# One attention block and a gated low-rank layer on one core: the last pair of heads takes its rounds upwards and projects four of its units beside itself

## What is computed

```python
q = (x @ wq.T + bq).reshape(B, S, H, hd)      # x is layernorm(x) here; k and v likewise
scores = einsum('bqhd,bkhd->bhqk', q, k) / sqrt(hd)
scores = where(causal, -inf, scores)
attn = einsum('bhqk,bkhd->bqhd', softmax(scores), v).reshape(B, S, D)
x = x + layernorm(attn @ wo.T + bo)
x = x + layernorm(gated_low_rank(layernorm(x)))   # 8 experts, one chosen for each token
```

## Time and profile before

| | us |
|---|---|
| median of 3 runs | 2445.38 |
| profiled execution, its own time | 2448.2 |
| its span, first to last instruction | 2446.4 |
| TensorE busy in the span | 2271.6 (93%) |
| ScalarE busy | 1728.8 (71%) |
| VectorE busy | 1673.9 (68%) |
| GpSimd busy | 1646.6 (67%) |
| mean granted clock of TensorE | 0.974 |

### The profile page before, as it was taken

One profiled execution on the slowest core, in us unless ns is written; L12 is line 12 of the kernel. 1 busy time (PEld: TensorE's weight loads), 2 busy tenths in 40 slices (PEclk: granted clock), 3 DMA queues, 4 the chain that ended last, 5 costly groups with the idle time before them and its releaser, 6 DMA issues. The chain is left out here.

```text
span 2446.4 us, 70598 instructions
## 1 busy us (share of the span) xinstructions
PE 2271.6 (93%) x28626; PEld 1446.4 (59%) x28626; DVE 1673.9 (68%) x4154; ACT 1728.8 (71%) x2355; POOL 1646.6 (67%) x1295
## 2 busy tenths in 40 slices
PE   4899999999999989899999999999997569999995
PEld 2566666675757666567575757666674335445452
DVE  8577777777777766476666666666666536777776
ACT  3477777777777766677777777777777746666665
POOL 4578788888888876678887888787887822222221
PEclk9999999999999999999999999999998779999997
DMA  9699999999999999999999999999999966656653
GB/s 239 130 195 203 200 200 202 202 205 203 204 202 205 203 197 199 199 194 191 185 189 182 185 185 186 185 180 184 174 177 191 204 142 155 160 154 169 156 155 86
DMA packets 1424676, 450.05 MB, mean 184 GB/s; under 512 B 1402048, under 2 KB 1402448, under 8 KB 1424352
## 3 DMA queue, kind: packets, MB, share of 16 engines
q1 hardware_dynamic: 1424352, 445.54, 98.5%
HBM read 67.95 MB, written 41.94 MB: 45 GB/s over the span
## 5 line engine op out<-in xcount | busy, mean ns | idle before, releaser
L911 POOL TENSOR_TENSOR hl<-probs,hl 128x1024 f16<-128x1024 f32 x544 | 1164.1, 2147 | 367.7 <-ACT hl L794 365.6
L787 ACT ACTIVATE probs<-s_ps,exp_bias 128x1024 f32<-128x1024 f32 (+7 forms) x768 | 632.7, 853 | 334.8 <-DVE exp_bias L636 328.2
L631 DVE TENSOR_REDUCE neg_max<-s_ps 128x1 f32<-128x1024 f32 (+7 forms) x768 | 676.1, 905 | 174.7 <-PE s_ps L472 174.6
L794 ACT ACTIVATE hl<-probs 128x1024 f16<-128x1024 f32 x544 | 575.0, 1057 | 70.1 <-DMA pt<-hl 53.9
L472 PE MATMUL s_ps<-nat 64*128 64x512 f16 (+3 forms) x3840 | 414.4, 354 | 75.7 <-ACT probs L787 72.3
L495 PE MATMUL o_ps<-v,pt 128*128 128x65 f16 x4352 | 434.8, 194 | 25.9 <-DMA pt<-hl 16.3
L495 PEld LDWEIGHTS o_ps<-v,pt 128*128 128x128 f16 x4352 | 403.5, 97 | 56.7 <-issue 23.2
L496 PE MATMUL o_ps<-v,pt 128*128 128x65 f16 x4352 | 434.9, 195 | 0.0
L497 PE MATMUL o_ps<-v,pt 128*128 128x65 f16 x4352 | 433.6, 193 | 0.0
L524 PE MATMUL u_ps<-arena,w 128*128 128x512 f16 x1008 | 385.8, 383 | 36.9 <-DMA arena<-hl 35.1
L496 PEld LDWEIGHTS o_ps<-v,pt 128*128 128x128 f16 x4352 | 402.7, 98 | 19.1
(11 more groups left out here) (160 smaller groups left out, 3672.0 us busy)
## 6 DMA issues: line engine op xcount, KB each, us to landing
w_raw<-in_w_pairs SPq DMA_DIRECT2D x48, 576.0 KB, 4.9
o_scratch<-o_hl SPq DMA_DIRECT2D x128, 128.0 KB, 2.5
out<-result SPq DMA_DIRECT2D x32, 512.0 KB, 3.3
x_in<-in_x SPq DMA_DIRECT2D x27, 512.0 KB, 4.9
pt<-hl SPq DMA_TRANSPOSE x544, 5.1
nat<-in_x SPq DMA_DIRECT2D x16, 512.0 KB, 4.6
xn_scratch<-xn SPq DMA_DIRECT2D x16, 512.0 KB, 4.1
xn<-in_x SPq DMA_DIRECT2D x11, 512.0 KB, 4.2
```

The source lines that it names most:

```text
L631: nc.vector.tensor_reduce(neg_max[:, step.round, acc, h:h + 1], s_ps[(n + h) % S_RING][:, first:end], AX_X, ALU.max, negate=True).then_inc ...
L787: last = nc.scalar.activation(probs_of(n)[:, cols], s_ps[n % S_RING][:, cols], ACT.Exp, bias=exp_bias[:, step.round, acc, h:h + 1], scale= ...
L794: nc.scalar.activation(hl_of(n, 0), probs_of(n), ACT.Copy).then_inc(p_hi_done, 1)
L911: nc.gpsimd.tensor_tensor(hl_of(n, 1), probs_of(n), hl_of(n, 0), ALU.subtract).then_inc(p_lo_done, 1)
```

## The change

- Pair 15 takes its rounds in the order of `FIRST_ROUNDS` (upwards), as pair 0 does.
- Eight of pair 15's units are projected during pair 14 (kind "prelast"), each over two steps, in steps 0 to 15. The last four, chunk 3 of k, chunks 0 and 3 of q and chunk 3 of v, are projected during pair 15 itself, in steps 0 to 4 (one, one, one and two steps).
- The weight blocks are summed by VectorE, in `center_wo`, with a reduction and a scaling; ScalarE's `wo_sum` is gone. Block k is summed and centred in body k + 2 (block 7 in body 10), and split by ScalarE and GpSimd in body k + 6, since the arena is in use until the units are done. The two fills of the arena move from body 0 to body 6.
- SyncE loads blocks 0 and 1 in body 0, block i + 1 in bodies 1 to 5, and block 7 in body 8. Of the smaller loads, five that `row_sum` needs are issued in body 7, the other six two a body in bodies 8 to 10 and awaited in body 15.
- `store_rows` stands one body later, in every pair.

```diff
-steps_of = lambda p: STEPS if p else FIRST_STEPS
-rounds_of = lambda p: ROUNDS if p else FIRST_ROUNDS
+upwards = lambda p: p in (0, PAIRS - 1)
+steps_of = lambda p: FIRST_STEPS if upwards(p) else STEPS
+rounds_of = lambda p: FIRST_ROUNDS if upwards(p) else ROUNDS
...
+UNITS["prelast"] = [("k", 0), ("k", 1), ("k", 2), ("q", 2), ("q", 1), ("v", 0), ("v", 1), ("v", 2), ("k", 3), ("q", 0),
+                    ("q", 3), ("v", 3)]
+LATE_UNIT = 8
...
+              "prelast": [2] * LATE_UNIT, "last": [1, 1, 1, 2]}
...
+units_of = lambda p: min(p + 1, PAIRS - 1)
...
-                    if i == half_done(p) + 1:
+                    if i == half_done(p) + 2:
                         store_rows(p, 0)
-                    if p > 0 and i == 1:
+                    if p > 0 and i == 2:
                         store_rows(p - 1, 1)
-                    if kind == "last" and i == 0:
+                    if kind == "last":
+                        for k in ([0, 1] if i == 0 else [i + 1] if i < KT - 2 else []):
+                            if k == 0:
+                                sp.wait_ge(s_done, NTASK * (PAIRS - 1))
+                            if k == 4:
+                                sp.wait_ge(pv_done, NTASK * (PAIRS - 1))
+                            if k == 6:
+                                sp.wait_ge(w_lo_done, 3 * PAIRS)
+                            sp.dma_start(wo_raw[k], fin["w_view"][k]).then_inc(wo_loaded[k], 16)
+                    if kind == "last" and i == KT - 1:
                         sp.wait_ge(unit_done, N_UNIT * PAIRS)
-                        sp.wait_ge(s_done, NTASK * (PAIRS - 1))
                         sp.wait_ge(mix_set, 2)
-
-                    if kind == "last" and i < KT:
-                        if i == 4:
-                            sp.wait_ge(pv_done, NTASK * (PAIRS - 1))
-                        if i == KT - 1:
-                            sp.wait_ge(wo_lo_done, 1)
-                        sp.dma_start(wo_raw[i], fin["w_view"][i]).then_inc(wo_loaded[i], 16)
-                    if kind == "last" and i >= KT:
-                        for tile, source in fin["loads"][4 * (i - KT):4 * (i - KT + 1)]:
+                        for tile, source in fin["row_loads"]:
+                            sp.dma_start(tile, source).then_inc(rows_loaded, 16)
+                    if kind == "last" and i == KT:
+
+                        sp.wait_ge(wo_lo_done, 1)
+                        sp.dma_start(wo_raw[KT - 1], fin["w_view"][KT - 1]).then_inc(wo_loaded[KT - 1], 16)
+                    if kind == "last" and KT <= i < KT + 3:
+                        for tile, source in fin["loads"][2 * (i - KT):2 * (i - KT + 1)]:
                             sp.dma_start(tile, source).then_inc(fin_loaded, 16)
...
             def center_wo(k):
-                raw = wo_raw[k]
+                raw, mean = wo_raw[k], wo_mean[:, k:k + 1]
+                dve.wait_ge(wo_loaded[k], 16)
+                nc.vector.tensor_reduce(mean, raw, AX_X, ALU.add).then_inc(wo_sum_done, 1)
+                dve.wait_ge(wo_sum_done, k + 1)
+                nc.vector.tensor_scalar(mean, mean, 1.0 / D, None, ALU.mult).then_inc(wo_mean_done, 1)
                 dve.wait_ge(wo_mean_done, k + 1)
-                nc.vector.tensor_scalar(raw, raw, wo_mean[:, k:k + 1], W_SCALE, ALU.subtract, ALU.mult).then_inc(
-                    wo_centered, 1)
+                nc.vector.tensor_scalar(raw, raw, mean, W_SCALE, ALU.subtract, ALU.mult).then_inc(wo_centered, 1)
...
-                        if 2 <= i < 2 + KT:
+                        if 2 <= i < 1 + KT:
                             center_wo(i - 2)
+                        if i == 10:
+                            center_wo(KT - 1)
...
             def wo_high(k):
                 act.wait_ge(wo_centered, k + 1)
+                act.wait_ge(unit_done, N_UNIT * PAIRS)
...
             def row_sum(n, row):
-                act.wait_ge(fin_loaded, 16 * len(fin["loads"]))
+                act.wait_ge(rows_loaded, 16 * len(fin["row_loads"]))
...
                 act.wait_ge(fin_centered, 3)
+                act.wait_ge(fin_loaded, 16 * len(fin["loads"]))
...
-                    if kind == "last" and 1 <= i < 1 + KT:
-                        wo_sum(i - 1)
-                    if kind == "last" and 2 <= i < 2 + KT:
-                        wo_high(i - 2)
+                    if kind == "last" and 6 <= i < 6 + KT:
+                        wo_high(i - 6)
...
-                    if kind == "last" and 2 <= i < 2 + KT:
-                        wo_low(i - 2)
+                    if kind == "last" and 6 <= i < 6 + KT:
+                        wo_low(i - 6)
```

More of the change, by code:

```diff
@@ L118 @@
 UNITS["first"] = UNITS["mid"]
-KIND = {0: "first", PAIRS - 1: "last", HALF_PAIRS - 2: "pre", HALF_PAIRS - 1: "turn"}
+UNITS["prelast"] = [("k", 0), ("k", 1), ("k", 2), ("q", 2), ("q", 1), ("v", 0), ("v", 1), ("v", 2), ("k", 3), ("q", 0),
+                    ("q", 3), ("v", 3)]
+LATE_UNIT = 8
+KIND = {0: "first", PAIRS - 1: "last", PAIRS - 2: "prelast", HALF_PAIRS - 2: "pre", HALF_PAIRS - 1: "turn"}
 order_of = lambda p: UNITS["start" if p == 0 else KIND.get(p - 1, "mid")]
@@ L125 @@
 UNIT_STEPS = {"first": [1, 1, 2, 2, 1, 1, 1, 2, 1, 2, 1, 2], "mid": [1, 1, 1, 2, 1, 2, 1, 2, 1, 2, 1, 2],
-              "pre": [1, 1, 1, 2, 1, 1, 1, 2, 2, 1, 2, 2], "turn": [1, 1, 1, 2, 1, 1, 1, 2, 2, 1, 2, 2], "last": []}
-UNIT_AT = {kind: [(u, i, n) for u, n in enumerate(counts) for i in range(n)] for kind, counts in UNIT_STEPS.items()}
-assert all(len(at) in (0, NSTEP) for at in UNIT_AT.values())
+              "pre": [1, 1, 1, 2, 1, 1, 1, 2, 2, 1, 2, 2], "turn": [1, 1, 1, 2, 1, 1, 1, 2, 2, 1, 2, 2],
+              "prelast": [2] * LATE_UNIT, "last": [1, 1, 1, 2]}
+UNIT_AT = {kind: [(u + (LATE_UNIT if kind == "last" else 0), i, n) for u, n in enumerate(counts) for i in range(n)]
+           for kind, counts in UNIT_STEPS.items()}
+units_of = lambda p: min(p + 1, PAIRS - 1)
 SPLITS = {"mid": {2: "q", 5: "k", 14: "v"}, "pre": {2: "q", 13: "k", 16: "v"}, "turn": {2: "q", 13: "k", 16: "v"}}
 SPLITS["first"] = {1: "v", 4: "q", 7: "k", 14: "v"}
-SPLITS["last"] = {}
+SPLITS["prelast"], SPLITS["last"] = {2: "q"}, {}
 last_step = lambda kind, m: max(i for i, (u, part, n) in enumerate(UNIT_AT[kind]) if UNITS[kind][u][0] == m)
@@ L265, in attend_phase @@
         fin_loaded = sem("fin_loaded")
+        rows_loaded = sem("rows_loaded")
         wo_loaded = [sem(f"wo_loaded{k}") for k in range(KT)]
@@ L269, in attend_phase @@
         ffn_hi_done = sem("ffn_hi_done")
+        wo_sum_done = sem("wo_sum_done")
         wo_mean_done = sem("wo_mean_done")
@@ L534, in body @@
                         scores(*step)
-                    if UNITS[kind]:
-                        u, part, count = UNIT_AT[kind][i]
-                        atoms = ATOMS[UNITS[kind][u][0]] // count
-                        project(p + 1, u, part * atoms, (part + 1) * atoms)
+                    for u, part, count in UNIT_AT[kind][i:i + 1]:
+                        atoms = ATOMS[order_of(units_of(p))[u][0]] // count
+                        project(units_of(p), u, part * atoms, (part + 1) * atoms)
                     for h in range(2):
@@ L719, in body @@
                     if kind == "last":
-                        if i == 0:
+                        if i == 6:
                             dve.wait_ge(unit_done, N_UNIT * PAIRS)
@@ L949, in body @@
                     for u in units_ending(kind, i - 1):
-                        unit_low(p + 1, u)
+                        unit_low(units_of(p), u)
                     if step:
@@ L1046, in finish_inputs @@
     fin["load_o"], fin["load_x"] = load_o, load_x
-    fin["loads"] = [(fin["bo_row"][:], b_o.partition_broadcast(P)),
-                    (fin["ffn_w"][:], by_block(ffn_in)),
-                    (fin["probe"][:], by_block(ffn_probe)),
-                    (fin["degen"][0:LOWS], ffn_mix[0:LOWS]), (fin["degen"][LOWS:P], ffn_mix[0:LOWS]),
-                    (fin["bias"][BIAS_HI:BIAS_HI + N_EXP], ffn_mix[LOWS:]),
-                    (fin["bias"][BIAS_LO:BIAS_LO + N_EXP], ffn_mix[LOWS:]),
+    fin["row_loads"] = [(fin["bo_row"][:], b_o.partition_broadcast(P)),
+                        (fin["degen"][0:LOWS], ffn_mix[0:LOWS]), (fin["degen"][LOWS:P], ffn_mix[0:LOWS]),
+                        (fin["bias"][BIAS_HI:BIAS_HI + N_EXP], ffn_mix[LOWS:]),
+                        (fin["bias"][BIAS_LO:BIAS_LO + N_EXP], ffn_mix[LOWS:])]
+    fin["loads"] = [(fin["ffn_w"][:], by_block(ffn_in)), (fin["probe"][:], by_block(ffn_probe)),
                     (fin["own"][:], own_in), (fin["rank"][:], rank_in),
```

12 lines of the change are left out of this document (4 added, 8 removed).

## The result

The changed kernel takes **2429.96 us**, the median of five runs (2426.13 to 2435.02), against 2444.70 (2442.43 to 2445.64) for the kernel before: a ratio of 0.9946, 95% interval 0.9931 to 0.9961. That is faster by 14.7 us by the medians and 13.2 by the ratio, where 34.3 were forecast. The same program was measured once more beside the experiments: 2432.85, ratio 0.9942 (0.9927 to 0.9956).

A forecast was written before the change was run, and what follows sets the result against it. It took TensorE to bound pair 14 and waits, with SyncE's in-order DMA queue behind the loads, to bound pair 15. Gains of 19.0 and 15.3 us sum to 34.3, giving 2411 us; range 2399 to 2429.

The forecast's parts named there:

- part 2: Units in pair 15's steps 0 to 4: TensorE's idle time covers them, costing little; 20.8 us if the cover were gone.
- part 3: Eight weight-block sums moved to VectorE in pair 15: zero cost, or 11 us if their cover goes.
- part 4: High and low parts four steps later in pair 15: engines alone would give 105 us to TensorE's last product.
- part 5: Loads spread in pair 15: the queue carries 99.0 us of work, so the pair takes 115, gain 15.3 us.
- part 1: Four units leave pair 14: it falls from 113.30 to 94.3 us, gain 19.0, with ends 92.5 and 105.2.
- side estimate of about 90 us: Pair 15's queue at the Trainium skill's transpose rate, 2.0 us each: about 90 us, under the engines' 105.
- The slower rival: Pair 15: VectorE waits for weight blocks ahead of the maxima and units are uncovered; 13 us slower, 2458; 3%.
- The last pair gains nothing: Pair 15 stays at 130 us as contention between loads and transposes grows when the queue is packed; 2426; 12%.
- Pair 14 is not freed: Pair 14 stays at 113 us if scores wait for exponentials each time; only 15.3 come, 2430; 5%.

The follow-up runs named there:

- the repeat: The changed kernel measured a second time with nothing edited, and its profiled execution (span 2432.3): 2432.85 us, ratio 0.9942 to the kernel before.
- the first execution: The profiled execution of the changed kernel's first measurement, the fastest of its five runs: 2426.13 us, span 2424.3.
- units back (second): Changed kernel with all twelve units in pair 14, none in pair 15, all k units ahead of q's: 2441.50 us, ratio 0.9978.
- weight loads small: Changed kernel with the eight output-weight loads cut from 512 KB to 8 KB, sums and subtractions reading another tile: 2428.38 us, ratio 0.9925.
- both gone: Changed kernel with 8 KB weight loads and also no sums by VectorE, zeros subtracted: 2428.30 us, ratio 0.9917.
- the two x loads: Changed kernel with both 512 KB loads of the last phase's x tiles issued in pair 10 instead of the last pair: 2430.42 us, ratio 0.9926.

## Why the prediction was wrong

The direction was right, and so was the reading that waits for loads held up the last pair. The size was wrong by a factor of over two. Of the 20.2 us that are missing in the repeat's trace, 13.7 are in pair 15, 4.5 in pair 14 and 2.0 outside both. Four steps failed: the cover of part 2, the zero of part 3, the time of part 4, and the queue's work of part 5, which part 1 had wrong in the same way.

**Part 1** was right in kind: 94.3 forecast, 98.3 and 98.8 measured, between its own ends of 92.5 and 105.2. Steps of half a unit do not wait for exponentials. The missing 4 us are in one row, TensorE's wait in the window of pair 14:

```profile
PE o_ps L514 <- DMA pt<-hl: 4.1, 2, 2.4
```

TensorE is busy for 93.43 of 98.33, which is the forecast within 1 us. Both waits end in the last 8 us of the pair: at the faster pace the transposes come late there, so the queue is already full when pair 15 begins. I had set the queue's work in pair 14 at 73 us by subtracting its waits. Summed from its single instructions it was 91.0 of the 113.30, and 94.0 of the 98.33 after the change. Part 5 counts work in the same way.

**Part 2** failed. The step was "its idle time is the cover". I took the cover from TensorE's 6.36 us of waiting ahead of one step of scores and from a mean over the pair, and spread the units over steps 0 to 4. In the kernel with the units back, round 0, which takes two of the four, has 9.33 us of which TensorE is busy for 5.96: there were 3.4 us of cover in it, where TensorE's busy time then rose by 11.9. In round 1 the cover was there. So the units cost 8.4 (5.6 by the first execution) of the 20.8 that the text gives for a missing cover.

**Part 3** failed too: "zero" was read from VectorE's 69.39 busy of 131.84. Seven of the eight sums come in consecutive bodies (2 to 8), and there the windows above show VectorE busy for 14.27 of 16.18, 14.70 of 14.98 and 12.99 of 13.75. One block by VectorE's timeline, and the subtraction of the next:

```profile
1869.40 1.21 DVE L696 TENSOR_REDUCE wo_mean<-nat 128x1 f32<-128x1024 f32 x1
1870.64 0.15 DVE L698 TENSOR_SCALAR wo_mean<-wo_mean 128x1 f32<-128x1 f32 x1
1870.83 2.32 DVE L700 TENSOR_SCALAR nat<-nat,wo_mean 128x1024 f32<-128x1024 f32 x1
...
1880.05 1.77 DVE L700 TENSOR_SCALAR nat<-nat,wo_mean 128x1024 f32<-128x1024 f32 x1
```

The reduction and the scaling are as forecast. The subtraction was priced at 0.75 and took 2.32: the block cost 3.7 us, not 2.1. All eight subtractions took 12.1 us after the change and 7.3 before. GpSimd's timeline over the same two blocks:

```profile
1870.47 2.13 POOL L928 TENSOR_TENSOR hl<-probs,hl 128x1024 f16<-128x1024 f32 x1 [1.65 <-ACT hl L817]
1872.57 1.60 POOL L933 TENSOR_TENSOR nat<-full,nat 128x512 f16<-128x512 f32 x1
...
1879.13 2.14 POOL L928 TENSOR_TENSOR hl<-probs,hl 128x1024 f16<-128x1024 f32 x1 [2.52 <-ACT hl L817]
```

GpSimd's low part ends at 1872.60 and the subtraction at 1873.15; the next low part ends at 1881.27 and the subtraction at 1881.82. In all eight blocks a GpSimd instruction ran when the subtraction began, and the subtraction ends 0.5 to 0.6 us after it, whenever it began (the shortest, 0.75, began when 0.14 of that instruction was left). So the subtraction stood behind GpSimd. The GpSimd instruction that follows the first one waits in turn: 1.60, where the same form takes 1.16 alone. Before the change seven of the eight subtractions began beside no GpSimd instruction and took 0.75. The Trainium skill (SBUF — State Buffer, section Who interferes with whom) says that VectorE and GpSimd share a pair of ports, which one instruction holds until it ends, and names this kind of VectorE instruction among those that can contend. The trace agrees. The prediction had weighed another rule of the Trainium skill, the one against reductions (VectorE: DVE Perf Modes, section Rules for kernel authors), and laid it aside. It bears on rounds 1 and 2, which are 2.4 and 3.7 us shorter with the sums on ScalarE, and not measurably on the total (0.9938 and 0.9942).

The slower rival, VectorE standing for a block ahead of the maxima, did occur once, for block 7 (4.6 us, 6.9 in the repeat), which waits for block 0's buffer.

**Part 4** came out too short. The forecast of 105 with 5 for the last transposes and products puts the last low part at 100 us after the pair's start. GpSimd's timeline:

```profile
1950.37 2.13 POOL L928 TENSOR_TENSOR hl<-probs,hl 128x1024 f16<-128x1024 f32 x1 [2.34 <-ACT hl L817]
```

It ends at 1952.50, 112.6 after the start. Some of this is the queue's, which reaches back to the engines when they need its buffers, so that no run here gives the engines' own time. It did not set the end alone: the queue issued the last transposes 4.9 us later still, as part 5 shows.

**Part 5** mis-sized the queue. Its timeline at the end of pair 15, and TensorE's last products:

```profile
1951.63 4.64 SPq L383 DMA_TRANSPOSE pt<-hl  x2
1956.32 0.94 SPq L1061 DMA_DIRECT2D xn<-in_x  x1
1957.36 5.88 SPq L383 DMA_TRANSPOSE pt<-hl  x2
...
1965.82 0.24 PE L514 MATMUL o_ps<-v,pt 128*128 128x65 f16 x1 [0.92 <-DMA pt<-hl]
```

The pair's length is the sum of four terms: from its start to the queue's first transpose whose low part is made in it (1851.99 here), the time that the queue's 59 instructions take from there to the last transpose, the gaps between them, and what follows the last one's end (1963.24). Summed from the single instructions of each trace:

| | start | 59 instructions | gaps | end | pair 15 |
|---|---|---|---|---|---|
| kernel before | 8.4 | 97.1 | 21.0 | 5.4 | 131.8 |
| forecast | 8.4 | 99.0 | 3 | 3.8 | 114.2 |
| changed | 12.1 | 104.6 | 6.6 | 4.1 | 127.4 |
| changed, repeat | 12.1 | 106.3 | 7.9 | 3.9 | 130.2 |
| units back (second) | 8.4 | 103.1 | 6.4 | 4.0 | 121.8 |
| weight loads small | 11.7 | 96.4 | 14.6 | 4.0 | 126.7 |
| both gone | 12.4 | 96.4 | 8.5 | 3.9 | 121.2 |

The forecast's row ends at TensorE's last product (3.8); to VectorE's read, as in the other rows, it would be 116. Its 99.0 still hold 1.9 us of small gaps.

The wait for low parts did go: 21.0 became 6.6, of which 3.9 are the 0.07 or so between any two instructions. But the same instructions took longer without it: the 28 transposes among them went from 71.9 (2.57 each) to 80.7 (2.88). Taking away 14.4 us of gaps brought 6.9. The 99.0 was a span less the idle time of the queue that issues, and the DMA engines were not idle in that time: their share over the pair was 0.99 with 21.0 us of gaps in it. By what path the gaps made the instructions shorter is not shown: before the change, the ten transposes that began behind a gap of over 0.3 us took 2.60 each and the other 18 took 2.55. Two rows could have warned. The DMA share was 0.99 over 131.84 us, and the same load in 115 us would have asked for 1.13, above the 1.11 of the fullest pair in the earlier trace rows; that is a warning and no limit, since pair 14 then ran at 1.16. And the 2.84 us a transfer of pair 7, which part 1 kept as its upper end, lies near the 2.88 and 2.94 that a transpose took here; part 5 did not use it. (Its side estimate of about 90 us by the Trainium skill's rate does not follow either: the 28 transposes at 2.0 each in place of 2.57 would leave 81 of the 97.1.)

The start is the other term that grew: at 1851.99 the low part of that transpose had been ready for 3.1 us, since the queue comes full out of pair 14. With the units back it is 8.4 again. The 8.4 us that the units cost divide here into 3.7 of start and 4.7 of the queue's own length.

The four terms are an account and not four causes. The row with the small weight loads shows it: eight transfers of 512 KB less take 9.9 us off the 59 instructions, and 6.7 of them come back as gaps, in rounds 1 to 4, where VectorE and TensorE set the time. Only with the sums gone too do the gaps stay at 8.5. What the queue sets by itself is the pair's second half, by the 3.1 to 4.5 us of the two x loads.

At the pair's very end the queue sets the time: the last low part is there at 1952.50, but the last transposes stand behind a pair of others and an x load and are issued from 1957.36 on, and TensorE's products follow them at once. The 34.7 us of waits for TensorE must not be read as waits for room: of the 28 transposes only two began right behind the products that had freed their room, the other 26 when the instruction ahead of them was done. The view names the last semaphore, not the cause. The prediction read the 16.6 of before in the same way, as time that might be slack.

**The rivals.** "The last pair gains nothing" (2426) is the nearest in mechanism: the last pair gained 1.6 to 4.4, for the reason that it gave, a queue that takes longer as it is packed, and for two that it did not give, the units and the sums. Its 12% were too little. "Pair 14 is not freed" named the measured number, 2430, by luck: it kept pair 14 at 113 and took 15.3 off pair 15, and the traces show nearly the reverse. The range ended at 2429, since each term of the forecast stood at its likely value and the rivals moved one thing at a time; in the table the start, the instructions and the gaps together are 12.9 to 15.9 us more than forecast.

What is left open: how the shortfall of pair 15 divides between TensorE, VectorE and the queue in rounds 1 to 4, where they cover each other; why the start of the program differs by 4 us between executions, and how much of the longer transposes comes from the other transfers beside them and how much from their following each other more closely.

## What to carry to other kernels

Read cover in the stage and not over the pair: 64 us of TensorE's idle time in the last pair held 3.4 us in the round where two of the four units went, and VectorE, busy for 53% of the last pair before the change, was busy for 88 to 98% of the three rounds that took most of its new work. The waits of a queue that issues transfers are not idle time of the engines that carry them; price a packed queue by a stretch that is packed, not by a half idle one less its waits. And where one bound stands behind another, removing either alone shows little: take both away in one kernel before a part is called harmless.

## What the runs showed of the hardware

- A full queue took 2.88 us a transpose of 512 KB in the mean of the 28 (2.94 in the repeat), and two of them with one load of 512 KB 6.6 to 7.3 us. From SyncE's timeline of the changed kernel:

```profile
1892.58 5.30 SPq L383 DMA_TRANSPOSE pt<-hl  x2
1897.94 1.13 SPq L432 DMA_DIRECT2D w_raw<-in_w_o  x1
1899.16 11.25 SPq L383 DMA_TRANSPOSE pt<-hl  x4
```

  The four in a row take 2.81 each; two and the load 6.58 from start to start. In the last rounds a 512 KB load less was 1.6 to 2.25 us less. The Trainium skill (DMA: Bandwidth & Descriptors, section Latency and other measured facts) gives 261 GB/s for a DMA transpose whose middle dimension is not contiguous, an estimated 2.0 us for this size; the rows show more, with what the engines carry beside the transposes in them.
- An issue instruction is not the transfer: from 1880 us on, a transpose of the changed kernel landed 4.3 to 8.4 us after its issue began, 5.1 in the middle, while the issue instructions took 1.8 to 4.5 us.
- A VectorE subtraction of 128 x 1024 float32 with a scalar for each row took 0.75 us alone. Begun while a GpSimd instruction ran, it ended 0.5 to 0.6 us after that one did, so it took up to 2.32. GpSimd's 128 x 512 difference took 1.16 alone and 1.60 behind it.
- The granted clock was 0.91 to 1.00 in the two rounds in which TensorE was full, 0.92 in round 2 with TensorE busy for 7.86 of 14.98, and 0.75 and 0.63 in round 3 and rounds 5 to 7, in which it was busy for 7.87 of 13.75 and 26.47 of 55.82. More work came with a higher clock: pair 15 without units ran at 0.74, with them at 0.79, and with 17.5 us more of TensorE's busy time it became only 8.4 longer.
